# One-hot lookups of a DLRM tower: ACT's one-hots in float32, fewer chunks split, indices first on SP

## The reference

```python
e = jnp.stack([tbl_f[ids[:, f]] for f in range(40)], axis=1)      # 512 x 40 x 32, float32
iidx, jidx = jnp.triu_indices(40, k=1)                             # 780 pairs of fields
z = jnp.einsum('bpd,pde,bpe->bp', e[:, iidx], bilinear_matrices, e[:, jidx])
h = jnp.concatenate([z, dense_ctx], axis=1)                        # 512 x 796
h = jnp.maximum(h @ W_top1 + b_top1, 0.0)                          # 796 x 512
h = jnp.maximum(h @ W_top2 + b_top2, 0.0)                          # 512 x 256
y = h @ W_top3                                                     # 256 x 1
```

## Time and profile before

| | us |
|---|---|
| median of 3 runs | 191.0 (190.97 to 191.17) |
| profiled execution | 191.4 |
| its span | 189.5 |
| PE busy | 174.3 (92%) |
| DVE busy | 147.9 (78%) |
| POOL busy | 107.0 (56%) |
| ACT busy | 52.9 (28%) |

### The profile page before, as it was taken

The page is one execution under the profiler, slowest core; times in us unless marked ns, Lnnn a source line. Parts: engine busy times, 40 slices in busy tenths (PEclk is TensorE's granted clock), DMA queues, the critical chain, the costliest instruction groups (busy, mean ns, idle before and its releaser), DMA issues.

```text
span 189.5 us, 3810 instructions
## 1 busy us (share of the span) xinstructions
PE 174.3 (92%) x1630; PEld 55.3 (29%) x1630; DVE 147.9 (78%) x147; ACT 52.9 (28%) x52; POOL 107.0 (56%) x114
## 2 busy tenths in 40 slices
PE   6578688999999999999989999999989999998992
PEld 6232232233322232232222222313222222222340
DVE  1799999997699889887958888888859897872502
ACT  3787496896100201102020102011120011112501
POOL 2587878877777777777777777778420002222000
PEclk9999999999999999999999999999999999999999
DMA  5996121340199500320000000000000000000000
GB/s 152 342 411 251 30 81 16 106 126 16 21 307 336 160 17 14 103 76 14 14 14 16 11 14 17 14 12 15 2 0 0 3 0 0 3 2 0 3 0 0
DMA packets 7609, 12.89 MB, mean 68 GB/s; under 512 B 2068, under 2 KB 4632, under 8 KB 7592
## 3 DMA queue, kind: packets, MB, share of 16 engines
q1 hardware_dynamic: 4376, 10.98, 16.5%
q0 software_dynamic: 3072, 1.58, 4.8%
q10 hardware_dynamic: 144, 0.08, 0.2%
HBM read 12.64 MB, written 0.00 MB: 67 GB/s over the span
## 4 chain that ended last, share of the span: by engine, by line
PE 85%; DVE 7%; issue 3%; DMA 3%; ACT 1%; DVEq 0%
PE ps_t L664 28%; PE ps_z L678 26%; PE ps_x L702 11%; PE ps_t L658 4%; PE ps_t L713 4%; DVE hot_dve L541 4%; PE ps_x L627 4%; PE ps_t L627 3%; DMA ids<-ids_oh 3%; PE ps_t L687 2%; PE ps_x L639 2%; DVE late_w L548 2%; PE ps_z L627 1%; DVE tbl_last L551 1%; DVE prod L581 1%
## 5 line engine op out<-in xcount | busy, mean ns | idle before, releaser
L581 DVE TENSOR_TENSOR prod<-ps_t,xt 128x1024 f32<-128x1024 f32 x100 | 116.1, 1217 | 22.3 <-PE ps_t L664 22.1
L470 POOL DMA_INDIRECT emb<-tbl,idx x96 | 95.8, 998 | 33.3 <-issue 29.0
L664 PE MATMUL ps_t<-xt,w_sb 32*128 32x512 f32 x360 | 56.0, 640 | 0.0
L678 PE MATMUL ps_z<-prod,ones 128*32 128x512 f32 x400 | 53.0, 604 | 0.0
L478 POOL TENSOR_TENSOR late_z<-late_z,tbl_oh 128x512 f32<-128x512 f32 x8 | 10.2, 1278 | 33.2 <-ACT tbl_oh L522 33.2
L664 PEld LDWEIGHTS ps_t<-xt,w_sb 32*128 32x128 f32 x360 | 18.0, 182 | 33.5 <-DVE prod L581 17.6
L702 PE MATMUL ps_x<-late_z,late_w 128*32 128x512 f32 x192 | 24.8, 592 | 0.0
L541 DVE TENSOR_SCALAR hot_dve<-ids,ramp 128x2048 bf16<-128x2048 int16 x26 | 18.2, 748 | 4.2 <-DMA ids<-ids_oh 4.2
L678 PEld LDWEIGHTS ps_z<-prod,ones 128*32 128x32 f32 x400 | 8.1, 108 | 37.9 <-issue 20.5
L493 ACT ACTIVATE hot_act<-ids,neg_ramp 128x2048 bf16<-128x2048 int16 x8 | 15.9, 1992 | 3.1 <-DMA ids<-ids_oh 3.1
L522 ACT ACTIVATE tbl_oh<-ps_x 128x512 f32<-128x512 f32 x8 | 4.8, 597 | 38.2 <-PE ps_x L702 38.2
(11 more groups left out here) (62 smaller groups left out, 86.1 us busy)
## 6 DMA issues: line engine op xcount, KB each, us to landing
ids<-ids_oh SPq DMA_DIRECT2D x4, 512.0 KB, 6.5
emb<-tbl,idx POOLq DMA_INDIRECT x96, 2.4
late_w<-w SPq DMA_DIRECT2D x1, 1280.0 KB
tbl_oh<-small_tables SPq DMA_DIRECT2D x2, 512.0 KB, 8.1
late_w<-w SPq DMA_DIRECT2D x2, 512.0 KB, 5.7
w_sb<-w_pairs SPq DMA_DIRECT2D x1, 704.0 KB, 4.1
tbl_oh<-small_tables SPq DMA_DIRECT2D x1, 640.0 KB
w_sb<-w_pairs SPq DMA_DIRECT2D x1, 640.0 KB, 3.8
```

What stands on the lines that cost most here:

```text
L470: nc.gpsimd.indirect_dma_start(emb[:, n % E_RING, t, u * D:(u + 1) * D], None, tables[field], bass.IndirectOffsetOnAxis(ap=idx[:, at:at + ...
L581: nc.vector.tensor_tensor(prod[:, g % PROD_RING, :].rearrange("p (i b) -> p i b", i=2), ps_t[PAIR[g]][:, :].rearrange("p (i b) -> p i b", ...
L664: last = nc.tensor.matmul(o, w_sb[s * D:(s + 1) * D, at:at + P], xt[s * D:(s + 1) * D, kk, :], start=True, stop=True)
L678: last = nc.tensor.matmul(ps_z[q * D:(q + 1) * D, :], ones[:, v * D:(v + 1) * D], prod[:, t // 2 % PROD_RING, t % 2 * B:(t % 2 + 1) * B], ...
```

## The change

Four edits:

- ACT's ring of one-hots, hot_act, is float32. PE multiplies such a chunk with the table's own float32 values, in four matmuls instead of twelve, and waits for the table's DMA (tbl_in) rather than for DVE's split.
- ACT's chunks are others, at the ends of the blocks (and the first one of block 4), so that in each part DVE's chunks lie side by side. DVE splits only those: split_chunks(n).
- The table's part 0 is 3 chunks, part 1 the other 5. Every chunk of DVE's now has a wait on tbl_last.
- The DMA of idx is issued first on SP, no longer on ACT.

```diff
-TBL_PARTS = [(0, 2), (2, OH_FIRST[1])] + [(OH_FIRST[j], OH_FIRST[j + 1]) for j in range(1, len(OH_BLOCKS))]
-ON_ACT = [(0, 3), (0, 6), (1, 5), (2, 3), (2, 6), (3, 1), (3, 4), (3, 7)]
+ON_ACT = [(0, 6), (0, 7), (1, 7), (2, 6), (2, 7), (3, 0), (3, 8), (3, 9)]
+TBL_PARTS = [(0, 3), (3, OH_FIRST[1])] + [(OH_FIRST[j], OH_FIRST[j + 1]) for j in range(1, len(OH_BLOCKS))]
+def split_chunks(n):
+    j = max(n - 1, 0)
+    own = [OH_FIRST[j] + c for c in range(OH_CHUNKS[j]) if (j, c) not in ON_ACT]
+    own = [at for at in own if TBL_PARTS[n][0] <= at < TBL_PARTS[n][1]]
+    assert own == list(range(own[0], own[-1] + 1))
+    return own[0], own[-1] + 1
...
-        hot_act = sb("hot_act", [P, ACT_RING, FB, B], BF16)
+        hot_act = sb("hot_act", [P, ACT_RING, FB, B])
...
+            sp.dma_start(idx[:, :], ids).then_inc(ids_in, 16)
             load_small_ids(0)
...
-            act.dma_start(idx[:, :], ids).then_inc(ids_in, 16)
...
-                cols = part_cols(n)
+                first, end = split_chunks(n)
+                cols = slice(first * FB * D, end * FB * D)
...
-                    if (j, c) == (0, TBL_PARTS[1][0]):
-                        pe.wait_ge(tbl_last_made, 2)
+                    if k not in ACT_HOTS and (j, c) != (0, 0):
+                        pe.wait_ge(tbl_last_made, PART_OF_BLOCK[j] + 1 if (j, c) >= (0, TBL_PARTS[1][0]) else 1)
+                    if (j, c) == (0, 0):
+                        pe.wait_ge(tbl_last_made, 1)
                     if c == 0:
-                        pe.wait_ge(tbl_last_made, PART_OF_BLOCK[j] + 1 if j else 1)
...
+                    if k in ACT_HOTS:
+                        parts = [tbl_oh[0:OH_P, cols]]
+                        pe.wait_ge(tbl_in[PART_OF_BLOCK[j]], 16)
...
-                                                    start=(c == 0 and part == 0), stop=(is_last_hot(k) and part == 2))
+                                                    start=(c == 0 and part == 0), stop=(is_last_hot(k) and part == len(parts) - 1))
```

More of the change, by code:

```diff
@@ L58 @@
 OH_FIRST = [sum(OH_CHUNKS[:j]) for j in range(len(OH_BLOCKS) + 1)]
-TBL_PARTS = [(0, 2), (2, OH_FIRST[1])] + [(OH_FIRST[j], OH_FIRST[j + 1]) for j in range(1, len(OH_BLOCKS))]
-PART_OF_BLOCK = [1 + j for j in range(len(OH_BLOCKS))]
 OH_FIELDS = []
@@ L69 @@
 WARM_UP = 11
-ON_ACT = [(0, 3), (0, 6), (1, 5), (2, 3), (2, 6), (3, 1), (3, 4), (3, 7)]
+ON_ACT = [(0, 6), (0, 7), (1, 7), (2, 6), (2, 7), (3, 0), (3, 8), (3, 9)]
 ACT_MAKES_FIRST, ACT_MAKES_AFTER = 2, {0: 1, 1: 2, 2: 1, 3: 2}
 assert len(ON_ACT) == ACT_MAKES_FIRST + sum(ACT_MAKES_AFTER.values())
+TBL_PARTS = [(0, 3), (3, OH_FIRST[1])] + [(OH_FIRST[j], OH_FIRST[j + 1]) for j in range(1, len(OH_BLOCKS))]
+PART_OF_BLOCK = [1 + j for j in range(len(OH_BLOCKS))]
+assert all((0, c) not in ON_ACT for c in range(TBL_PARTS[0][1]))
+def split_chunks(n):
[4 more added lines that the diff above has]
+    return own[0], own[-1] + 1
 ORDER = []
```

## The result

Five runs of each: the changed kernel takes 193.2 us (191.97 to 193.67), the one before 191.17 (190.97 to 191.91). The ratio is 1.0099, 95% interval 1.0072 to 1.0126. The forecast was 191.3, and its range ended at 192.2. The profiled execution, 191.97 us with a span of 190.1, is the shortest of the five, and only 0.6 us longer than the profile of before; the spans of the others are 190.3 to 191.6, and the mean granted clock of PE is 0.987 to 0.990 in all five, against 0.999 in the profile of before. One execution in what follows, 195.28 us with the changed kernel measured again, lies over 1.5% above the fastest of its kernel: the medians in us count it, the ratios and the counts of executions don't.

The account below looks back on a forecast made before the run. DVE's one-hots and table splits set the pace until 33 us, PE after 38 us. Block 2 -0.39, block 4's float32 chunks +0.63 and waits +0.05 make +0.3 us on 191.0: 191.3 us, range 190.4 to 192.2.

Parts of the forecast that it names:

- ACT's float32 passes: ACT's two passes for a one-hot take 2.0 and 1.9 us in float32, no change from bfloat16.
- the chunk: A float32 chunk on PE takes 0.86 us, 0.21 more than bfloat16; three of them in block 4 add 0.63.
- the second waits on PE: PE's second wait for each DVE chunk, long met after block 0, costs 0.05 us in all.
- step 6: Block 2: ACT is the bound, the copy comes 0.39 us earlier at 31.76, and DVE's savings end as idle time.
- (a): On PE, the float32 chunk costs 1.00 us, not 0.86: total 192.0 us; chance 0.16.
- (c): PE's waits cost issue time: +0.25 us more, total 191.6 us; chance 0.09.
- (d): On PE, the float32 chunk streams at 0.65 us: total 190.2 us; chance 0.10.
- (e): At the start, ids_oh, no longer sharing with ACT's queue, lands 0.4 us sooner: total 190.6 us; chance 0.07.
- the term for the landing of ids_oh: At the start, idx first on SP makes ids_oh land 0.3 us later, between bounds of no shift and 0.9.
- Rival (b): At the start, ids_oh lands 0.8 us later instead of 0.3, behind all of idx: total 191.8 us; chance 0.12.
- I see it in time by 0.2 us: At the start, the table's first part, 64 KB longer, still lands 0.2 us before it is needed.
- rival (f): PE's clock falls to 1.2 GHz in a 2.2 us pause before the first chunk: +4 us, 195 us; chance 0.03.

Follow-up runs that it names:

- gathers held: The changed kernel with POOL waiting for ids_oh(0) as well as idx before its first gather: 193.1 us, ratio 1.0107.
- idx second: The changed kernel with the DMA of idx on SP behind ids_oh(0) instead of ahead of it: 191.04 us, ratio 0.9995.
- the longer warm-up: The changed kernel with 22 instead of 11 matmuls on the identity ahead of the first chunk: 192.15 us, ratio 1.0051.
- the first experiments: The changed kernel measured again unedited, 192.49 us (1.0067), then with 22 instead of 11 warm-up matmuls, 192.15 us (1.0051).

## Why the prediction was wrong

**What held.** In the profile of the change the steps behind the landing of ids_oh held. Counted from the landing of ids_oh, the forecast was -0.25 us at block 1's copy, -0.69 at block 2's, +0.63 through block 4, and 0 in sum. Measured, with the landing 0.64 later: block 1's copy at 22.70, 0.40 - 0.64 = -0.24; block 2's at 32.15, 0.00 - 0.64 = -0.64; block 4's chunks +0.6; and 183.7 us behind the start in both. ACT's float32 passes (1.91), the chunk (0.86 us; (3,8) and (3,9) below, 1.83 us to the next group at 50.84, with a change of tile shape in it) and the second waits on PE came as costed:

```profile
49.01 1.90 PE L646 MATMUL ps_x<-hot_act,tbl_oh 125*32 125x512 f32 x16
```

The bound of block 2 is ACT, as step 6 has it: from the copy of block 1 to 30.98 the chain runs through ACT's passes. Rivals (a), (c) and (d) fall by these rows, and (e) since ids_oh landed later and not sooner. Something like what (e) had in mind exists, but it takes idx behind ids_oh and not ahead of it: the kernel before gained 0.5 us that way.

**The step that failed is the first, the term for the landing of ids_oh**: "I take +0.3, nearest to the issue time less what idx took of the engines before". ids_oh landed 0.58 to 1.18 us later than in the profile of before, in four profiles of kernels with the changed order (6.33, 6.87, 6.51 and, gathers held, 6.27). The issue is 0.46 of it. The rest, 0.1 to 0.7 us, comes with what stood ahead of it in the queue: the one line on the kernel before costs 1.6 us, another load ahead costs 1.3, and with idx behind ids_oh the cost is gone. The inside of that is not shown. With idx first the first slice, 4.75 us, moves 111 GB/s, not 152 as in the earlier trace rows:

```profile
GB/s 111 367 405 276 17 94 20 102 124 16 18 294 352 161 14 14 79 100 17 11 14 17 14 14 10 17 14 3 5 0 0 3 0 0 3 0 2 0 0 0
```

My argument was that the bytes are the same and idx shared the engines with ids_oh before too, so that only part of the issue counts. It rested on a wrong reading of the earlier trace rows: 0.72 MB is "just" the sum of three transfers by chance, since ids_oh landed only 0.95 us after the end of that slice. By then 0.99 MB had moved in the kernel before (174 GB/s over 5.69 us), and 0.98 MB when it landed in the change (155 GB/s over 6.33 us). The engines had other loads in flight beside it in both, and 0.72 MB says nothing of what idx took. What the runs show is the queue: after issue ids_oh needed 3.9 to 4.95 us with nothing ahead of it in SP's queue, and 5.1 to 5.7 with idx or the weights ahead. Rival (b), +0.8 instead of +0.3, was the likelier value, though its 191.8 is still 1.4 us short of what was measured. My upper bound of 0.9, worked out as issue plus bytes at 152 GB/s, was itself too low by 0.3 for one execution.

**A second term of that step failed too**, seen with idx on ACT: "I see it in time by 0.2 us", of the table's first part. In the change, and with idx second, no wait for it shows in the profile. With idx on ACT the landing isn't in the way, and the rest of the change was forecast at 0 in sum. It measured 0.55 us slower than before (1.0029), with DVE waiting 0.20 us for that part in one profile and 0.60 in another. What the other tenths are isn't settled.

**The third miss is rival (f)**, given 0.03. The pause before the first chunk grew to 2.72 us, more than the 2.2 forecast since ids_oh was late, and the clock was fallen in all five executions of the first measurement and in 14 of 27 later ones with something ahead of ids_oh and the old warm-up. Over the profiles it stood at 0.83 or 0.66 in the first stretch where that pause was 2.3 to 2.7 us (five profiles), and at 1.00 where it was 1.7 us or less. Nor was the kernel before quite free of it: 7 of its 91 executions beside the experiments have a mean clock of 0.991, and their spans are 189.8 to 190.1, where the others' median is 189.2 to 189.4. The Trainium skill, "TensorE: Matmul & The Clock Gate", HAM oscillation, warned of idle gaps, and this trace now agrees: groups at 0.43 instead of 0.22 us from 8.3 to 11.2. Its price was far less than the 4 us I gave, as the slow stretch ended before all of block 0 was done. In the profile of the change it cost nothing: PE works without a pause from 8.30 us and comes to block 1's first chunk at 15.47, just when DVE is done with the split that this chunk waits for.

```profile
14.32 1.09 DVE L566 TENSOR_TENSOR tbl_last<-late_w 128x896 bf16<-128x896 f32 x1
...
15.47 0.40 PE L646 MATMUL ps_z<-hot_dve,tbl_oh 125*32 125x512 bf16 x4
```

With the longer warm-up and a full clock it is the same span behind the start, 183.7. By the median of executions with and without it the fallen clock costs 0.5 us in the changed kernel and 0.6 with idx first on the kernel before, and in the profiles with 0.66, where the slow stretch lasts longer (to 15.0 us with idx first on the kernel before), 0.9 to 1.1. The first and the third miss come from one line of the diff. A warm-up that lasts to the first chunk keeps the clock full, the order on SP mends both.

In sum, on the chip of the first experiments: changed kernel +1.4 us; some 0.3 of it the clock, by the longer warm-up (its interval reaches nothing); the other microsecond goes with the late landing, which was 0.82 us in the profile with the longer warm-up. Idx back on ACT returns only 0.8 us, and there DVE waits for the table's first part; idx second returns 1.4. Why the first measurement shows 0.6 us more than that chip (193.2 against 192.5; the intervals of the ratios overlap) isn't settled; its five executions all had the fallen clock, and I have a profile of only the shortest.

## What to carry to other kernels

Issue first, with nothing ahead of it in its queue, the load that the first instruction of the pacing engine waits for. In this kernel every tenth by which it landed later was in the total. Then look at the next load: the table's first part, which the change made longer, was waited for with one place of idx and not with another. A faster format or a shorter split pays only in the stretch that its engine paces: float32 one-hots cost 0.21 us each where PE sets the pace, and are likely to gain a few tenths in all where DVE or ACT does. A change of several edits can hide a good one: the new places of ACT's chunks alone gain 0.3 us. When a change lengthens the wait before an engine's first work, look at the granted clock of many executions, not of one profile.

## What the runs showed that I had not expected

A small transfer at the head of the queue cost the one behind it more than its issue: with 80 KB or 128 KB ahead, ids_oh landed 5.1 to 5.7 us after issue, against 3.9 to 4.7 with idx behind it. With the same 80 KB beside it, from ACT's queue, it took 4.5 to 4.95. And idx itself, at the head, was there for POOL at 2.99 us instead of 6.14, 3 us sooner, which nothing in this kernel could use; a lead of 0.23 us from ACT's queue did the same (2.92).
